# Three half chunks instead of two turned by VectorE, and products of E one pair later

## The chip, the cores and the metric

One core of a Trainium2 chip runs the whole program. The metric is the time of one execution in device microseconds, as the median of several runs. Some names: TensorE is PE in the profile (its weight loads are PEld), VectorE is DVE, ScalarE is ACT, GpSimd is POOL, SyncE is SP; SP issues nearly all transfers, and they run on the core's 16 DMA engines.

## The reference, cut to what matters

Four graph layers over 5120 nodes with 64 features share one dense 5120 x 5120 matrix `adj` of float32 (105 MB). Each layer normalises `x`, and then:

```python
# layer 0, with e made from the normalised x
h = adj @ (adj.T @ e)
x = x + layernorm(h) * gamma + beta + h_in
# layer 1:  x = x + adj @ h
# layer 2:  out = h @ w0; T1 = adj @ h; T2 = 2 adj @ T1 - h; T3 = 2 adj @ T2 - T1; x = x + (out + ...) + bias
# layer 3:  degree = sum of each row of (adj + I); x = x + relu(d * (adj + I) * d @ (h @ W + b))
```

The change touches layer 0 alone. There `adj` is needed both as it lies in memory (for `adj.T @ e`) and turned (for `adj @ t`). The later layers need only the turned form.

## The kernel before, in words

`adj` has 10 blocks of 512 rows; two blocks make a pair of rows, so there are 5 pairs (`ROWS`). The columns are cut into 7 groups g (`NG`): groups 0 to 5 have 768 columns (6 chunks of 128), the last has 512 (4 chunks). All work of layer 0 goes group by group, and in a group pair by pair.

For every pair (g, m):

- SP loads the two blocks of the pair into `raw` (1.5 MB each, `load_next`, L582; 1 MB each for group 6). `raw` holds one whole group, so block m of group g+1 may be loaded only when block m of group g has been turned and its row sums taken.
- The pair is turned into `staged`. Each chunk of 128 columns gives two half chunks, so a pair has 12. From the third pair on (`VECTOR_FROM`) TensorE turns ten of them, four 128 x 128 transposes each (`turn_banks`, L673), through four banks of PSUM (`turned`), and ScalarE copies each bank into `staged` (`copy_banks`, L879). VectorE turns the last chunk, that is two half chunks, straight from `raw` into `staged` with 16 transposes of 32-row blocks (`turn_chunk`, L1129).
- SP stores the turned pair, 3 MB, to `adj_t` in HBM (`store`, L570). `staged` has room for two pairs, so pair p may be turned into it only when the store of pair p - 2 has landed and its products are done (`wait_stage_free`).
- TensorE multiplies the turned pair with `t_cur`, the part of `adj.T @ E` of this group (`product_for_h`, L640), into `acc`, and VectorE adds that to `h_acc` (`add_h`, L1083).
- TensorE multiplies both raw blocks of the same pair of the next group with `E` into `t_acc` (`products_for_t`, L651). After the last one ScalarE copies `t_acc` out (L914), TensorE turns it (L716) and ScalarE writes `t_cur` (L931).

Row sums of the raw blocks (`sum_rows`) are taken by ScalarE (L923) or VectorE (L1040). Those of groups 1 to 5 are ScalarE's. Of group 6, VectorE takes one for each pair while group 5 is worked on, and two at the start of group 6.

Everything is ordered by hand. In iteration (g, i) of `group(g)` TensorE does: turn the next pair, multiply pair (g, i) with `t_cur`, multiply pair i of group g + 1 with `E`. VectorE does: turn its part of the next pair, its row sums if any, then `add_h(g, i)`. ScalarE does: copy the banks of the next pair, then its row sums. SP does: load the first block (g+1, 2m) after `wait_turned`, which asks for TensorE's and for VectorE's part of the turning, then store the pair, then load the second block. All three stand in one queue of SP, and each waits for those ahead of it. Group 6 has an order of its own (`last_group`), in units of half a pair; nothing in it is turned by VectorE, and it begins when `adj.T @ E` of group 6 is complete. After it come the passes of the later layers, whose tiles are loaded from `adj_t` (L588).

Of the kernel before, what the change touches and what calls it, by code (L numbers as in the profile page):

```python
# [33 lines left out]
PASSES = 5  # L34
MOVED_BANK = 3
VECTOR_FROM, VECTOR_LAST = 2, 0
VECTOR_CHUNKS = 1
EARLY_SLOTS = 1
LATE_SLOTS = 4
SLOTS = EARLY_SLOTS + NB + LATE_SLOTS  # L40
# [196 lines left out]
def gnn_stack(nc, x_d, adj_d, wu_d, du_d, pu_d, wi_d, di_d, pi_d, gam_d, bet_d, w2_d, b2_d, w3_d, b3_d, out_d):  # L237
    plan = Plan()
    ctx = ExitStack()
    with ctx:  # L240
# [178 lines left out]
        def chunks(g):  # L419

            return CHUNKS_LAST if g == NG - 1 else CHUNKS
# [36 lines left out]
        def by_vector(g, m):  # L458

            return m < VECTOR_LAST if g == NG - 1 else pair_no(g, m) >= VECTOR_FROM  # L460

        def banks(g, m):

            return range(2 * chunks(g) - 2 * VECTOR_CHUNKS * by_vector(g, m))

        def is_moved(g, m, j):

# [167 lines left out]
        def _(pe):  # L635
# [9 lines left out]
            def products_for_t(g, m):  # L645

                pe.wait_ge(raw_in[m], g * 16 + 16)
                columns = chunks(g) * P // 2
                for a in range(SUB):
                    for h in range(2):  # L650
                        last = nc.tensor.matmul(t_acc[h * D:(h + 1) * D, 0:columns], E[:, m * SUB + a, :],  # L651
                                                raw_of(g, m)[:, a, h * columns:(h + 1) * columns],
                                                start=(m == 0 and a == 0), stop=(m == NB - 1 and a == SUB - 1))
                if m == NB - 1:
                    last.then_inc(t_done, 1)
# [8 lines left out]
            def turn_banks(g, m, some):  # L664

                for j in some:
                    n = TURN_NO[g, m, j]
                    if n >= TURN_BANKS:
                        wait_bank(TURNS[n - TURN_BANKS])
                    c, h = divmod(j, 2)  # L670
                    for a in range(SUB):
                        b, sub = divmod(2 * a + h, SUB)
                        last = nc.tensor.transpose(turned[n % TURN_BANKS][:, a * P:(a + 1) * P],  # L673
                                                   raw_of(g, 2 * m + b)[:, sub, c * P:(c + 1) * P], ident[:, :])
                    last.then_inc(chunk_turned, 1)
# [61 lines left out]
            def group(g):  # L737
                for i in range(ROWS):
                    after = (g, i + 1) if i + 1 < ROWS else (g + 1, 0)
                    begun = BEGUN if (g, i) == (0, 0) else 0  # L740
                    turn_banks(*after, range(begun, TURN_BANKS))
                    if i == 0:
                        turn_t(g)
                    turn_banks(*after, banks(*after)[TURN_BANKS:])
                    if i == 0:
                        pe.wait_ge(t_ready, g + 1)
                    wait_copied(pe, g, i)
                    for u in (2 * i, 2 * i + 1):
                        product_for_h(g, u)
                    for m in (2 * i, 2 * i + 1):  # L750
                        products_for_t(g + 1, m)

            def last_group():
                g = NG - 1
                for u in range(UNITS):
                    if u + 2 < UNITS:
                        turn_unit(g, u + 2, range(CHUNKS_LAST))
                    if u == 0:
                        turn_t(g)
                        pe.wait_ge(t_ready, g + 1)  # L760
                    if u >= 2 and u % 2 == 0:
                        rows_of_h(u // 2 - 1)
                    wait_copied(pe, NG - 1, u // 2, u % 2)
                    product_for_h(g, u)
# [252 lines left out]
        def _(dve):  # L1017
# [94 lines left out]
            def turn_chunk(g, m):  # L1112

                if by_vector(g, m):
                    for b in range(2):
                        dve.wait_ge(raw_in[2 * m + b], g * 16 + 16)
                    if g < NG - 1:
                        wait_stage_free(dve, g, m)
                    elif m >= 1:
                        wait_turned(dve, g, m - 1)  # L1120
                    else:
                        wait_turned(dve, g - 1, ROWS - 1)
                    half, c = chunks(g) // 2, chunks(g) - 1
                    rows = raw_flat if g < NG - 1 else raw_flat[:, 0:NB * SUB * CHUNKS_LAST * P]
                    src = rows[:, :].rearrange("p (m a h k) -> p m h a k", m=ROWS, h=2, k=chunks(g) * P)[:, m]
                    dst = turned_into(g, 2 * m + 1)[:, (half - 1) * PAIR:half * PAIR].rearrange("p (h a n) -> p h a n", h=2, a=SUB)
                    for q in range(4):
                        for b in range(4):
                            last = nc.vector.transpose(dst[b * SQ:(b + 1) * SQ, :, :, q * SQ:(q + 1) * SQ],  # L1129
                                                       src[q * SQ:(q + 1) * SQ, :, :, c * P + b * SQ:c * P + (b + 1) * SQ])  # L1130
                    last.then_inc(vector_turned, 1)

            def group(g):
# [189 lines left out]
```

## Time and profile before

| what | us |
|---|---|
| median of 3 runs (lowest, highest) | 1450.26 (1450.21, 1451.71) |
| the profiled execution's own time | 1449.24 |
| its span, first to last instruction | 1447.0 |
| PE busy | 1419.3 (98%) |
| DVE busy | 491.5 (34%) |
| ACT busy | 399.7 (28%) |
| POOL busy | 84.2 (6%) |
| TensorE's granted clock, share of full | 0.999 |

Busy time is what the engine's instructions cover; matmuls are pipelined and their ends are modelled, so a PE that is busy all the time is not at its peak. The span of 1447.0 us has two parts here: layer 0 with the turning, up to about 550 us, and the passes after it. DMA share is the mean busy share of the 16 DMA engines; since packets overlap a little it can read above 1.

### The profile page before, as it was taken

Reading aid. Unit: us, or ns where it says so; the run is one execution under the profiler, and the core shown is the slowest. Engines: PE = TensorE matmul, PEld = TensorE weight load, DVE = VectorE, ACT = ScalarE, POOL = GpSimd, SP = SyncE. Lnnn points to the kernel's source line nnn. Section 1 sums busy time; section 2 is a strip of 40 time slices with the busy share of each in tenths; the row PEclk is TensorE's granted clock in tenths of the full one; section 3 lists DMA queues with packets and bytes.
Section 4 is the critical chain, followed back from the end, with each engine's and each line's share of the span. In section 5 each row is a group of like instructions: output and inputs, shape, how many; then the busy total and the mean of one; then the engine's idle time right before and its main releaser. Section 6 shows DMA issues by size and latency. Waiting matters only on the chain.

```text
span 1447.0 us, 18473 instructions
## 1 busy us (share of the span) xinstructions
PE 1419.3 (98%) x7601; PEld 600.1 (41%) x7601; DVE 491.5 (34%) x1082; ACT 399.7 (28%) x885; POOL 84.2 (6%) x67
## 2 busy tenths in 40 slices
PE   6999999999999999999999999999999999999998
PEld 3555555555555563333333333333333333333332
DVE  6684544545546533331132211011311121101044
ACT  2378777777776551000000000000000000000000
POOL 2210000000000037000000000000000000000000
PEclk9999999999999999999999999999999999999999
DMA  9999999999999998999996797899797848996998
GB/s 322 392 417 411 420 412 414 419 408 415 401 406 372 388 403 348 419 421 420 420 413 217 315 361 291 327 350 319 302 340 263 311 180 354 393 382 224 357 420 315
DMA packets 97607, 523.26 MB, mean 362 GB/s; under 512 B 18764, under 2 KB 18804, under 8 KB 54644
## 3 DMA queue, kind: packets, MB, share of 16 engines
q1 hardware_dynamic: 90436, 520.40, 91.3%
q10 hardware_dynamic: 7088, 1.67, 0.5%
q8 instruction: 61, 1.00, 0.3%
q14 instruction: 22, 0.18, 0.0%
HBM read 415.88 MB, written 106.17 MB: 361 GB/s over the span
## 4 chain that ended last, share of the span: by engine, by line
PE 61%; DMA 2%; DVE 1%; POOL 0%; issue 0%; ACT 0%; DVEq 0%
PE turned L640 33%; PE acc L640 25%; DMA over_wide<-adj_t 2%; PE turned L673 1%; PE turned L825 1%; PE t_rows L809 0%; PE turned L831 0%; DVE staged L1169 0%; PE t_acc L799 0%; PE t_acc L725 0%; PE t_rows L725 0%; POOL rstd L1272 0%; DVE staged L1035 0%; DVE staged L1025 0%; DVE staged L1231 0%
## 5 line engine op out<-in xcount | busy, mean ns | idle before, releaser
L1129 DVE STREAM_TRANSPOSE staged<-raw 32x256 f32<-32x256 f32 x448 | 194.9, 435 | 5.8
L651 PE MATMUL t_acc<-raw,E 128*64 128x384 f32 (+1 forms) x1120 | 184.4, 476 | 5.7 <-DMA raw<-in_adj_dram 5.7
L879 ACT ACTIVATE staged<-turned 128x512 f32<-128x512 f32 x303 | 152.7, 640 | 105.7 <-PE turned L673 105.2
L923 ACT ACTIVATE t_t<-raw 128x768 uint8<-128x768 f32 (+1 forms) x216 | 177.2, 902 | 0.0
L640 PE MATMUL acc<-staged,t_cur 128*64 128x512 f32 x720 | 161.1, 596 | 0.0
L673 PE MATMUL turned<-ident,raw 128*128 128x128 f32 x1376 | 160.2, 274 | 0.0
L673 PEld LDWEIGHTS turned<-ident,raw 128*128 128x128 f32 x1376 | 149.7, 140 | 24.9 <-issue 24.9
L640 PE MATMUL turned<-over_last,C 128*64 128x512 f32 x672 | 152.1, 592 | 0.0
L651 PEld LDWEIGHTS t_acc<-raw,E 128*64 128x64 f32 x1120 | 78.3, 138 | 109.4 <-issue 86.0
L1272 POOL TENSOR_TENSOR rstd<-rstd,minus_half 128x8 f32<-128x8 f32 (+1 forms) x30 | 44.2, 1473 | 1267.1 <-DVE rstd L1031 1267.1
L640 PE MATMUL turned<-over_last,R 128*64 128x512 f32 x512 | 116.5, 593 | 0.0
L640 PE MATMUL acc<-over_last,R 128*64 128x512 f32 x440 | 99.9, 593 | 0.0
L987 ACT ACTIVATE part<-turned 128x512 f32<-128x512 f32 x12 | 7.2, 597 | 313.1 <-PE turned L640 287.3
L1169 DVE STREAM_TRANSPOSE staged<-staged 32x128 f32<-32x128 f32 x304 | 91.9, 302 | 4.5
L640 PEld LDWEIGHTS turned<-over_last,C 128*64 128x64 f32 x672 | 48.2, 137 | 95.5 <-issue 95.5
L1083 DVE TENSOR_TENSOR h_acc<-acc,h_acc 128x512 f32<-128x512 f32 x30 | 20.8, 692 | 197.2 <-PE acc L640 197.2
L640 PEld LDWEIGHTS acc<-staged,t_cur 128*64 128x64 f32 x720 | 49.0, 137 | 90.8 <-issue 90.8
L640 PE MATMUL acc<-over_last,C 128*64 128x512 f32 x384 | 86.6, 592 | 0.0
L1243 DVE TENSOR_TENSOR staged<-turned,part 128x512 f32<-128x512 f32 x11 | 7.6, 692 | 225.8 <-PE turned L640 191.7
L640 PE MATMUL turned<-over_last,E 128*64 128x512 f32 x320 | 74.1, 593 | 0.0
L640 PEld LDWEIGHTS turned<-over_last,R 128*64 128x64 f32 x512 | 36.2, 137 | 71.2 <-issue 69.4
L855 ACT ACTIVATE staged<-staged 128x512 f32<-128x512 f32 x10 | 6.3, 630 | 206.0 <-DVE staged L1025 206.0
(139 smaller groups left out, 1062.9 us busy)
## 6 DMA issues: line engine op xcount, KB each, us to landing
over_last<-adj_t SPq DMA_DIRECT2D x181, 1024.0 KB, 8.9
staged<-adj_t SPq DMA_DIRECT2D x91, 1024.0 KB, 9.5
raw<-in_adj_dram SPq DMA_DIRECT2D x60, 1536.0 KB, 19.7
adj_t<-staged SPq DMA_DIRECT2D x30, 3072.0 KB, 18.1
over_wide<-adj_t SPq DMA_DIRECT2D x23, 1024.0 KB, 7.6
raw<-in_adj_dram SPq DMA_DIRECT2D x10, 1024.0 KB, 14.8
adj_t<-over_last SPq DMA_DIRECT2D x8, 1024.0 KB, 12.1
adj_t<-C SPq DMA_DIRECT2D x2, 1024.0 KB, 21.7
```

The costliest lines, as they stand in the source:

```text
L640: last = nc.tensor.matmul(bank[h * D:(h + 1) * D, :], v[:, t + c, :], tile[:, (2 * c + h) * B:(2 * c + h + 1) * B], start=start and c == 0 ...
L651: last = nc.tensor.matmul(t_acc[h * D:(h + 1) * D, 0:columns], E[:, m * SUB + a, :], raw_of(g, m)[:, a, h * columns:(h + 1) * columns], st ...
L673: last = nc.tensor.transpose(turned[n % TURN_BANKS][:, a * P:(a + 1) * P], raw_of(g, 2 * m + b)[:, sub, c * P:(c + 1) * P], ident[:, :])
L825: last = nc.tensor.matmul(weigh_bank[odd][:, i * 4 * D:(i + 1) * 4 * D], feat_t[rows, nodes], w0123[rows, :, :].rearrange("p w d -> p (w d ...
L879: nc.scalar.activation(turned_into(g, u)[:, i * B:(i + 1) * B], turned[n % TURN_BANKS][:, :], ACT.Copy) \
L923: nc.scalar.activation(passed[n % 2][:, 0:chunks(g) * P], raw_of(g, m)[:, a, :], ACT.Copy, accum_out=deg_part[:, m * SUB + a, g:g + 1]).th ...
L987: nc.scalar.activation(part[:, m, :], open_bank[plan.bank["dual", p, m]], ACT.Copy).then_inc(part_saved, 1)
L1083: ins = nc.vector.tensor_tensor(h_acc[:, m, :], acc[pair % 2][:, :], h_acc[:, m, :], ALU.add)
L1129: last = nc.vector.transpose(dst[b * SQ:(b + 1) * SQ, :, :, q * SQ:(q + 1) * SQ], src[q * SQ:(q + 1) * SQ, :, :, c * P + b * SQ:c * P + (b ...
L1169: last = nc.vector.transpose(dst[b * SQ:(b + 1) * SQ, :, h, e, :], src[q * SQ:(q + 1) * SQ, :, b, :])
L1243: ins = nc.vector.tensor_tensor(y_sb[r % 2], bank, part[:, m, :], ALU.add)
L1272: op.tensor_tensor(v, v, minus_half[:, t(0)], ALU.pow).then_inc(pow_ready, 1)
```

## The change: what it does

`VECTOR_CHUNKS` goes. A new `vector_banks(g, m)` says how many half chunks of a pair are VectorE's: 3 in groups 1 to 5, 2 in group 0 (pairs from the third on) and none in group 6. TensorE turns the rest (`banks`): 9 half chunks instead of 10 for the 25 pairs of groups 1 to 5. VectorE does the whole last chunk as before, then the second half of the chunk before it with 16 more transposes of half the width.

TensorE's products of `E` with pair i of group g + 1 move from iteration (g, i) to iteration (g, i + 1). Those of the last pair (blocks `NB - 2` and `NB - 1`) move to the start of the next group, ahead of the turning there; that is the same place in TensorE's order as before, but the products of the pair before now stand directly ahead of them.

```diff
+        def vector_banks(g, m):
+            if not by_vector(g, m):
+                return 0
+            return 3 if 0 < g < NG - 1 else 2
+
         def banks(g, m):
-            return range(2 * chunks(g) - 2 * VECTOR_CHUNKS * by_vector(g, m))
+            return range(2 * chunks(g) - vector_banks(g, m))
...
                 for i in range(ROWS):
                     after = (g, i + 1) if i + 1 < ROWS else (g + 1, 0)
                     begun = BEGUN if (g, i) == (0, 0) else 0
+                    if i == 0 and g > 0:
+                        products_for_t(g, NB - 2)
+                        products_for_t(g, NB - 1)
                     turn_banks(*after, range(begun, TURN_BANKS))
...
                     for u in (2 * i, 2 * i + 1):
                         product_for_h(g, u)
-                    for m in (2 * i, 2 * i + 1):
-                        products_for_t(g + 1, m)
+                    if i > 0:
+                        products_for_t(g + 1, 2 * i - 2)
+                        products_for_t(g + 1, 2 * i - 1)
 
             def last_group():
                 g = NG - 1
+                products_for_t(g, NB - 2)
+                products_for_t(g, NB - 1)
...
-                    half, c = chunks(g) // 2, chunks(g) - 1
...
-                    dst = turned_into(g, 2 * m + 1)[:, (half - 1) * PAIR:half * PAIR].rearrange("p (h a n) -> p h a n", h=2, a=SUB)
-                    for q in range(4):
-                        for b in range(4):
-                            last = nc.vector.transpose(dst[b * SQ:(b + 1) * SQ, :, :, q * SQ:(q + 1) * SQ],
-                                                       src[q * SQ:(q + 1) * SQ, :, :, c * P + b * SQ:c * P + (b + 1) * SQ])
+                    half = chunks(g) // 2
+                    left = vector_banks(g, m)
+                    c = chunks(g) - 1
+                    while left > 0:
+                        at = (c - half) * PAIR
+                        dst = turned_into(g, 2 * m + 1)[:, at:at + PAIR].rearrange("p (h a n) -> p h a n", h=2, a=SUB)
+                        for q in range(4):
+                            for b in range(4):
+                                to = dst[b * SQ:(b + 1) * SQ, :, :, q * SQ:(q + 1) * SQ]
+                                of_raw = src[q * SQ:(q + 1) * SQ, :, :, c * P + b * SQ:c * P + (b + 1) * SQ]
+                                if left == 1:
+                                    to, of_raw = to[:, 1], of_raw[:, 1]
+                                last = nc.vector.transpose(to, of_raw)
+                        left, c = left - 2, c - 1
                     last.then_inc(vector_turned, 1)
```

## Rows read from the trace of the kernel before

**Rows 1.** The page: data rate in 40 slices of 36.2 us.

```profile
GB/s 322 392 417 411 420 412 414 419 408 415 401 406 372 388 403 348 419 421 420 420 413 217 315 361 291 327 350 319 302 340 263 311 180 354 393 382 224 357 420 315
```

**Rows 2.** Windows between stores' issues: length, busy per engine, clock, DMA share, GB/s.

```profile
94.52:169.74 75.22, 75.22 (x485) 41.64 (x483) 41.68 (x87) 58.65 (x133) 0.00 (x0) 1.00 1.02 416
169.74:261.67 91.93, 90.86 (x581) 49.64 (x579) 45.41 (x102) 70.21 (x159) 0.00 (x0) 1.00 1.02 415
261.67:431.38 169.71, 167.71 (x1064) 90.77 (x1062) 83.23 (x187) 128.86 (x291) 0.00 (x0) 1.00 1.01 410
431.38:488.84 57.46, 55.78 (x389) 33.17 (x387) 36.67 (x71) 38.81 (x91) 0.00 (x0) 1.00 0.98 373
```

**Rows 3.** Timeline of PE, one pair of group 3: start, length, work, [idle before].

```profile
327.16 2.75 PE L651 MATMUL t_acc<-raw,E 128*64 128x384 f32 x16
330.09 2.80 PE L651 MATMUL t_acc<-raw,E 128*64 128x384 f32 x16 [0.18 <-DMA raw<-in_adj_dram]
332.82 4.59 PE L673 MATMUL turned<-ident,raw 128*128 128x128 f32 x40
337.34 5.37 PE L640 MATMUL acc<-staged,t_cur 128*64 128x512 f32 x24
```

**Rows 4.** Waits from 80 to 508 us: total us, times, longest.

```profile
PE t_acc L651 <- DMA raw<-in_adj_dram: 4.7, 15, 0.9
```

**Rows 5.** Timeline of SP's queue in the same pair.

```profile
337.44 0.37 SPq L582 DMA_DIRECT2D raw<-in_adj_dram  x1
338.55 0.34 SPq L570 DMA_DIRECT2D adj_t<-staged  x1
338.99 0.37 SPq L582 DMA_DIRECT2D raw<-in_adj_dram  x1
```

**Rows 6.** DMA issues at 337.44, 338.55, 338.99: size, us from issue to landing.

```profile
raw<-in_adj_dram SPq DMA_DIRECT2D x1, 1536.0 KB, 11.9
adj_t<-staged SPq DMA_DIRECT2D x1, 3072.0 KB, 18.4
raw<-in_adj_dram SPq DMA_DIRECT2D x1, 1536.0 KB, 21.8
```

**Rows 7.** Lines: form, count, busy us, mean ns (L1169 from 787 to 793 us).

```profile
L1169 DVE STREAM_TRANSPOSE staged<-staged 32x128 f32<-32x128 f32 x16 | 4.8, 302 | 0.2
L673 PE MATMUL turned<-ident,raw 128*128 128x128 f32 x1376 | 160.2, 274 | 0.0
```

**Rows 8.** Timeline of DVE in group 5.

```profile
451.53 0.69 DVE L1083 TENSOR_TENSOR h_acc<-acc,h_acc 128x512 f32<-128x512 f32 x1 [8.16 <-PE acc L640]
452.14 7.17 DVE L1129 STREAM_TRANSPOSE staged<-raw 32x256 f32<-32x256 f32 x16
459.35 2.29 DVE L1040 TENSOR_REDUCE deg_part<-raw 128x4 f32<-128x2048 f32 x1
```

**Rows 9.** Timelines of SP's queue and PE at the end of group 5.

```profile
487.73 0.37 SPq L582 DMA_DIRECT2D raw<-in_adj_dram  x1
488.84 0.65 SPq L570 DMA_DIRECT2D adj_t<-staged  x1
489.59 0.38 SPq L582 DMA_DIRECT2D raw<-in_adj_dram  x1
508.08 1.95 PE L651 MATMUL t_acc<-raw,E 128*64 128x256 f32 x16 [0.96 <-DMA raw<-in_adj_dram]
```

**Rows 10.** DMA issues at 475.46, 487.73, 488.84, 489.59 and, alone in the queue, 1150.45.

```profile
raw<-in_adj_dram SPq DMA_DIRECT2D x1, 1024.0 KB, 18.9
raw<-in_adj_dram SPq DMA_DIRECT2D x1, 1024.0 KB, 9.4
adj_t<-staged SPq DMA_DIRECT2D x1, 3072.0 KB, 15.8
raw<-in_adj_dram SPq DMA_DIRECT2D x1, 1024.0 KB, 18.4
staged<-adj_t SPq DMA_DIRECT2D x1, 1024.0 KB, 4.7
```

More of the change, by code:

```diff
@@ L36 @@
 VECTOR_FROM, VECTOR_LAST = 2, 0
-VECTOR_CHUNKS = 1
 EARLY_SLOTS = 1
```

## The prediction

> **What bounds the kernel now.** The page says PE 98% busy, and one would stop there. The data rate by slices [rows 1] says something else: until slice 12 the transfers run near the 419 to 421 GB/s that the load-only stretch from slice 17 on reaches. So I cut layer 0 into windows that begin and end at issues of a store, one store per pair [rows 2]. The first holds 5 pairs (15.04 us each), the next 6 (15.32), the third 11 (15.43), the fourth, group 5 with its smaller loads, 4 (14.37). The DMA share is 1.01 to 1.02 in the first three, 0.98 in the fourth.
>
> Next PE's timeline of one pair [rows 3]. Steps start 4.52 us apart for the 40 transposes (332.82 to 337.34), about 5.2 for the 24 products with `t_cur` (5.37 long, the next overlapping), and 5.66 for the 32 products with `E` (327.16 to 332.82), with a wait for a `raw` block between its halves. By itself PE needs the 15.04 us a pair of the first window, where it was busy for 75.22 of 75.22 us [rows 2]. Later it takes 15.4 for the same work, and what stops it are those waits for `raw`, 4.7 us in 15 pieces by the list of waits [rows 4], some more where only the weight loads waited.
>
> Is the block late because it was asked for late? SP's queue and the landings answer [rows 5, 6]. First load, store and second load are issued at 337.44, 338.55 and 338.99 and land at 349.3, 356.95 and 360.8; the second load of the pair before (same row, one period of 15.4 earlier) landed at 345.4. So the landings follow one another by 3.9, 7.6 and 3.9 us, 15.4 together, and the first load stood in the queue for 8.0 us before its turn. The queue is never empty: PE is held to the pace of the transfers, 6.29 MB a pair, and was near it before. That is the bound from about 200 us to the end of group 5.
>
> The phase ends with it too [rows 9, 10]: the last raw load of group 6 is issued at 489.59 and lands at 508.0, and PE, idle for 0.96 us, starts its last products with `E` at 508.08. `t_cur` of group 6, and all that follows, hang on this landing.
>
> **The change part by part.** *Transposes and copies taken away.* 25 pairs lose 4 transposes each, 100 in all, at 4.52 / 40 = 0.113 us: 11.3 us of PE (by busy time per instruction, 160.2 / 1376 = 0.116, 11.6 us) [rows 3, 7]. PE then needs 15.04 - 0.45 = 14.6 us a pair. ScalarE loses 25 copies. What hides it: the transfers at 15.1 to 15.4 a pair. Value on the path: 0. Its bounds are 0 and -11.6 us, the second if PE were the bound. I take 0 since the nearest row, 8.0 us of queue ahead of each first load, excludes that earlier turning lands anything earlier.
>
> *Products of E one pair later.* Nothing is added or removed; PE has a pair more before it needs a block, so its 4.7 us of waits go [rows 4]. What is late next: `staged` has two places, so turning pair p waits for the landing of store p - 2, and this comes at the transfers' pace. Blocks of the last pair keep their place, so the wait at 508.08 stays. Value 0, bounds 0 and -4.7 us.
>
> *VectorE's third half chunk.* 16 transposes of 32x128. The form stands in the passes: 302 ns each, 16 in 4.8 us busy plus 0.2 idle, 5.0 us [rows 7]; the source there lies closer together than the stretches of `raw` do, and the 16 of twice the width take 7.17 [rows 8], so between 4.8 and 7.2 us. I take 5.0; turning is then 12.2 us. Who waits: `last` releases SP, where first load, store and second load of the pair stand behind `wait_turned`, and PE's products with `t_cur`.
>
> In groups 1 to 4 VectorE has 12.2 + 0.7 of 15.4 us, and starts when the store two pairs before has landed. Counted from there, the queue still holds second load, first load, store, second load: 3.9 + 3.9 + 7.6 + 3.9 = 19.3 us [rows 6]. The load that waits for VectorE is issued at 12.2, 7 us ahead of need. At a group's start PE has two pairs of products in a row, then none; VectorE waits for `add_h` about 1.5 us longer there, which leaves over 3 us even with ScalarE's row sums in the way. Cost 0; if that cover were gone, each us late is a us of the end.
>
> Group 5 is different: loads are 1 MB, VectorE also sums rows, and the queue is shorter. VectorE needs 12.2 + 2.3 + 0.6 = 15.1 us a pair [rows 8] where the transfers need 14.4 [rows 2]. Its chain: `add_h(5,0)` ends at 451.53 + 0.69 = 452.2, less 0.5 since PE turns one half chunk less just before, 451.7. Turning (5,2) ends at 463.9, (5,3) at 479.0, (5,4) at 494.1; the second sets the load of 479.1, which the queue reaches at about 481, the third the first load of the last pair, 494.2 instead of 487.73 [rows 9]. The queue reaches it when the load of 475.46 has landed, 494.4 [rows 10], so it is issued just as its turn comes, and a load into an empty queue takes 4.7 us from issue to landing for 1 MB [rows 10], against 2.7 for one in line (494.4 to 487.73 + 9.4 = 497.1). It lands at 494.2 + 4.7 = 498.9, up to 499.2 as its packets are smaller. The store takes 7.5 us in line (497.1 to 488.84 + 15.8 = 504.6), the last load 3.4 (to 489.59 + 18.4 = 508.0). So the end is 499.0 + 7.5 + 3.4 = 509.9, less 0.2 because engines that ran dry start together: 509.7, against 508.0. Cost +1.7 us. Bounds: 0, where the queue holds, and +8: 16 transposes at 7.2 us instead of 5.0 add 2.2 in each of three turnings, 6.6, less what the queue still hides.
>
> The added instructions are 16 for VectorE in each pair; they and PE's 8 fewer (weight loads too) leave the work of the queue as it was, 0.
>
> **Sum.** 0 + 0 + 0 + 1.7 on the profiled 1449.24 us (span 1447.0 and 2.2 around it): 1450.9. The median is 1.0 above the profiled execution, so 1450.26 + 1.7 = 1452.0 us.
>
> A rule that speaks against "transfers are at their limit": the Trainium skill, DMA: Bandwidth & Descriptors, Specifications, gives 435 GB/s as the ceiling of the fabric. By it a pair's 6.29 MB would take 14.5 us, PE at 15.0 would have been the bound all along, and PE's saving would come through, up to 11 us. The windows show 410 to 416 GB/s at a share over 1, so the measurement decides; the rule adds weight to the fourth rival alone.
>
> **The rivals.**
>
> *A, the forecast:* groups 1 to 4 unchanged, group 5 gives 1 to 3 us back. 1452.0, its own range 1450 to 1454.
>
> *B, slower:* VectorE's chain in group 5 lets the queue run dry for two pairs. It decides once the turning takes over 12.6 us or so: then the load at 479.1 is late as well, and each dry spell costs 4.7 - 2.7 = 2.0 us on top of the lag. With 13 us a turning: 3 x 0.8 + 2.0 more, 1452.0 + 4.4, about 1456. For it: the strided source, and 2 us between 479.1 and 481, which is just what a load needs to start. Against: 302 ns is a measured form, and engines are in line long before.
>
> *C, faster:* the pace of 15.4 instead of 15.1 is itself a consequence of PE's waits, and goes with them. The 11 pairs of the third window at 15.04 instead of 15.43 and the 6 of the second instead of 15.32 [rows 2] give 4.3 + 1.7 = 6.0, less 1.7 in group 5: 1446.0. For it: the first window ran at 15.04 with the same packets [rows 2]. Against: loads stand 8.0 us in line, so no wait of PE reaches the transfers.
>
> *D, faster:* PE is the bound, as the page's 98% has it. 11.3 us and the 4.7 of waits, 16 together, at least the 11.3: 1434 to 1439. Against: every row of the queue.
>
> *E, nothing:* the change takes and gives nothing that ends up on the path, VectorE being hidden in group 5 as well: 1450.3. It is also the case that the change doesn't do what it says for the time.
>
> **How the numbers follow.** No change means within 0.2%, 2.9 us, so 1447.4 to 1453.2. A has 0.52, of which 0.07 lies over 1453.2; B 0.17; C 0.14, of which 0.12 is under 1447.4; D 0.05; E 0.12. Faster: 0.17. Slower: 0.07 + 0.17 = 0.24. No change: 0.59. The range 1445.5 to 1456 leaves out D, a third of C and nearly half of B, 0.05 + 0.05 + 0.07.
>
> **What would show it.** Windows of groups 1 to 4 with 15.3 to 15.5 us a pair and a share over 1, PE's waits there turned from `raw` into waits for ScalarE's copies, that is for a store, and no or few waits for `raw` inside a group; VectorE's 32 transposes in 12.2 us; in group 5 a first load of the last pair issued at about 494 and the last landing at 509.7. C shows as pairs of 15.1 us in group 3, D as pairs of 14.5. I am wrong if the last landing comes before 507 or after 512, or if the passes, which nothing here touches, change by more than 1 us.

## The result, and the profile after

| | median of runs (lowest, highest) | profiled execution | its span | clock |
|---|---|---|---|---|
| before | 1450.26 (1449.39, 1452.03), 11 runs | 1449.24 | 1447.0 | 0.999 |
| after | 1458.7 (1453.91, 1461.57), 11 runs | 1455.46 | 1453.7 | 0.995 |

The ratio is 1.0053 (95%: 1.0044 to 1.0062): slower by about 8 us (6.4 to 9.0), where 1452.0 with a range of 1445.5 to 1456.0 was predicted. The profiled execution of after lies in the lower part of its runs; the places of the loss can be read from it, the size comes from the medians. The experiments have 5 to 11 timed runs each; in their sessions before had 1450.8, and differences are taken from that.

The page after, its totals, its data rate (36.3 us a slice) and the group of VectorE's transposes:

```profile
PE 1412.3 (97%) x7501; PEld 591.8 (41%) x7501; DVE 613.9 (42%) x1482; ACT 387.3 (27%) x860; POOL 84.3 (6%) x67
...
GB/s 320 395 416 412 408 404 399 413 374 411 417 413 359 365 417 360 420 421 420 420 420 201 322 358 295 349 330 316 298 351 264 302 185 360 387 380 230 352 419 316
...
L1148 DVE STREAM_TRANSPOSE staged<-raw 32x256 f32<-32x256 f32 (+1 forms) x848 | 316.4, 373 | 49.0 <-DMA adj_t<-staged 37.8
```

The work moved as written: PE has 7 us less, VectorE 122 us more. But nine of the slices 3 to 14 carry less than in [rows 1], 359 and 365 in slices 13 and 14 against 372 and 388; only slices 4, 11 and 12 carry more.

Windows between the same stores as in [rows 2], with 5, 6, 11 and 4 pairs (length, busy per engine, clock, DMA share, GB/s):

```profile
91.47:169.86 78.39, 77.37 (x487) 41.12 (x485) 64.07 (x152) 60.17 (x139) 0.00 (x0) 1.00 1.01 409
169.86:265.17 95.31, 91.20 (x573) 48.28 (x571) 74.98 (x199) 68.19 (x156) 0.00 (x0) 1.00 1.01 406
265.17:435.44 170.27, 164.40 (x1016) 87.09 (x1014) 137.36 (x364) 123.38 (x279) 0.00 (x0) 0.98 1.01 405
435.44:497.63 62.19, 57.91 (x401) 33.87 (x397) 54.14 (x135) 33.05 (x79) 0.00 (x0) 1.00 0.95 364
```

They come to 15.7, 15.9, 15.5 and 15.5 us a pair instead of 15.04, 15.32, 15.43 and 14.37. Their borders are issues, and an issue may come early and land at the old time: the first window begins 3 us earlier than before's for that reason. Landings tell it more cleanly. The last raw block of each group landed at (us, from the transfers in both traces):

| end of group | 0 | 1 | 2 | 3 | 4 | 5 |
|---|---|---|---|---|---|---|
| before | 130.3 | 207.4 | 283.9 | 360.8 | 438.5 | 508.0 |
| after | 130.5 | 208.8 | 286.9 | 365.3 | 441.5 | 514.2 |

Of the 6.7 us that the span grew, 6.2 are there at the last landing: 3.0 gathered in groups 1 to 4, of which I had said 0, and 3.2 in group 5, of which I had said 1.7. The rest is TensorE's slower start after its last wait; what follows it is within 1 us of before.

The net hides two opposite movements. Add up the gaps between landings for each kind of transfer (first load, store, second load of a pair). In groups 1 to 4 the 20 first loads took 84.2 us against before's 77.9, but the 20 stores took 149.1 against 152.4. In group 5 the first loads took 21.4 against 14.5, the second loads 13.4 against 16.8. So late first loads cost 13.2 us in all, and other transfers that landed more quickly gave 7 of them back. Many stores land 7.3 us behind their forerunner and many 7.6, in every trace; what decides between the two, no run here separates. In group 4 after even gained 1.5 us on before.

Waits of after from 80 to 521 us (total us, times, longest):

```profile
DVE staged L1148 <- DMA adj_t<-staged: 37.8, 17, 3.8
DVE h_acc L1094 <- PE acc L645: 26.1, 6, 6.9
...
PE t_acc L656 <- DMA raw<-in_adj_dram: 11.7, 5, 3.8
...
PE turned L678 <- ACT staged L890: 5.7, 6, 1.0
```

Inside a group PE's small waits for `raw` are gone, as predicted. In their place stand five large ones, 11.7 us against the 4.7 of [rows 4], one at the end of each of groups 1 to 5, where the blocks of the last pair keep their old place. One of them in PE's timeline (start, length, work, [idle before]):

```profile
276.02 7.91 PE L656 MATMUL t_acc<-raw,E 128*64 128x384 f32 x48
286.92 5.39 PE L656 MATMUL t_acc<-raw,E 128*64 128x384 f32 x16 [3.00 <-DMA raw<-in_adj_dram]
292.24 2.26 PE L678 MATMUL turned<-ident,raw 128*128 128x128 f32 x16
...
294.66 2.35 PE L678 MATMUL turned<-ident,raw 128*128 128x128 f32 x20
296.94 5.37 PE L645 MATMUL acc<-staged,t_cur 128*64 128x512 f32 x24
```

So the lateness of the transfers is saved up over a group and paid in one piece. What makes them late is seen on the two sides of one late load. VectorE, and SP's queue, at the start of group 3:

```profile
283.21 12.24 DVE L1148 STREAM_TRANSPOSE staged<-raw 32x256 f32<-32x256 f32 x32 [2.77 <-DMA adj_t<-staged]
302.36 0.69 DVE L1094 TENSOR_TENSOR h_acc<-acc,h_acc 128x512 f32<-128x512 f32 x1 [6.91 <-PE acc L645]
302.96 12.24 DVE L1148 STREAM_TRANSPOSE staged<-raw 32x256 f32<-32x256 f32 x32
```

```profile
298.59 17.04 SPq L587 DMA_DIRECT2D raw<-in_adj_dram  x2
315.72 0.46 SPq L575 DMA_DIRECT2D adj_t<-staged  x1
```

PE had two pairs of products with `E` to do in a row (276.02 to 292.3), then turned, and only then came to the products with `t_cur` (296.94). `add_h` hangs on these, and VectorE's next turning stands behind `add_h`. It stood idle for 6.9 us (the longest of six such waits, 26.1 us in all) and turned from 302.96 to 315.2. The store that freed its place had landed at 298.1, so the start was 4.9 us later than the transfers allowed. The next load was issued at 315.3 (the last 0.37 us of the piece beginning at 298.59), while the load ahead of it, issued at 298.59, landed 19.3 us later, at 317.9. It had 2.7 us in line. It landed 7.6 us after its issue, at 322.9, that is 4.9 us after its forerunner and not the 3.9 of the full queue [rows 6].

VectorE in group 5:

```profile
454.14 0.69 DVE L1094 TENSOR_TENSOR h_acc<-acc,h_acc 128x512 f32<-128x512 f32 x1 [4.08 <-PE acc L645]
454.75 12.23 DVE L1148 STREAM_TRANSPOSE staged<-raw 32x256 f32<-32x256 f32 x32
467.01 2.29 DVE L1051 TENSOR_REDUCE deg_part<-raw 128x4 f32<-128x2048 f32 x1
469.21 0.68 DVE L1094 TENSOR_TENSOR h_acc<-acc,h_acc 128x512 f32<-128x512 f32 x1
469.81 12.23 DVE L1148 STREAM_TRANSPOSE staged<-raw 32x256 f32<-32x256 f32 x32
...
484.87 12.23 DVE L1148 STREAM_TRANSPOSE staged<-raw 32x256 f32<-32x256 f32 x32
```

SP's queue there, and PE at the end:

```profile
483.12 14.41 SPq L587 DMA_DIRECT2D raw<-in_adj_dram  x2
497.63 0.46 SPq L575 DMA_DIRECT2D adj_t<-staged  x1
```

```profile
514.26 3.25 PE L656 MATMUL t_acc<-raw,E 128*64 128x256 f32 x16 [3.78 <-DMA raw<-in_adj_dram]
```

The chain of turning, sums and `add_h`, 15.06 us a pair (454.75, 469.81, 484.87), has the lengths that I gave it. It began 3.1 us later than forecast (454.75 instead of 451.7), and group 5 itself had begun 3.0 us late. The first load of the last pair was issued at 497.17 instead of 494.2 and landed 6.4 us later, at 503.6, where 4.7 were counted [rows 10].

### The profile page after: what moved, and what is told of

It is laid out like the page before. It is cut to its first block, busy times and chain, and to the rows that moved or that the text cites. A ratio compares the mean times of both kernels' runs of the same rounds, so it can differ in the third digit from the quotient of the medians.

```text
span 1453.7 us, 18648 instructions
## 1 busy us (share of the span) xinstructions
PE 1412.3 (97%) x7501; PEld 591.8 (41%) x7501; DVE 613.9 (42%) x1482; ACT 387.3 (27%) x860; POOL 84.3 (6%) x67
## 4 chain that ended last, share of the span: by engine, by line
PE 61%; DVE 2%; POOL 0%; issue 0%; ACT 0%; DVEq 0%
PE turned L645 33%; PE acc L645 26%; DVE staged L1188 1%; PE turned L678 1%; PE turned L836 1%; PE t_rows L820 0%; PE turned L842 0%; POOL rstd L1291 0%; PE t_acc L810 0%; PE t_acc L730 0%; DVE staged L1046 0%; DVE staged L1036 0%; DVE X L1234 0%; DVE staged L1264 0%; DVE rstd L1041 0%; DVE total L1035 0%
## 5 line engine op out<-in xcount | busy, mean ns | idle before, releaser
L1148 DVE STREAM_TRANSPOSE staged<-raw 32x256 f32<-32x256 f32 (+1 forms) x848 | 316.4, 373 | 49.0 <-DMA adj_t<-staged 37.8
L656 PE MATMUL t_acc<-raw,E 128*64 128x384 f32 (+1 forms) x1120 | 183.9, 481 | 11.7 <-DMA raw<-in_adj_dram 11.7
L890 ACT ACTIVATE staged<-turned 128x512 f32<-128x512 f32 x278 | 140.7, 642 | 80.2 <-PE turned L678 79.8
L678 PE MATMUL turned<-ident,raw 128*128 128x128 f32 x1276 | 153.2, 277 | 7.6 <-ACT staged L890 5.7
L678 PEld LDWEIGHTS turned<-ident,raw 128*128 128x128 f32 x1276 | 138.7, 141 | 39.0 <-issue 27.4
L1262 DVE TENSOR_TENSOR staged<-acc,part 128x512 f32<-128x512 f32 x8 | 5.5, 691 | 151.5 <-PE acc L645 83.3
L645 PEld LDWEIGHTS turned<-over_last,R 128*64 128x64 f32 x512 | 36.2, 137 | 71.2 <-issue 70.6
## 6 DMA issues: line engine op xcount, KB each, us to landing
raw<-in_adj_dram SPq DMA_DIRECT2D x10, 1024.0 KB, 12.3
```

The costliest lines, as they stand in the source:

```text
L645: last = nc.tensor.matmul(bank[h * D:(h + 1) * D, :], v[:, t + c, :], tile[:, (2 * c + h) * B:(2 * c + h + 1) * B], start=start and c == 0 ...
L890: nc.scalar.activation(turned_into(g, u)[:, i * B:(i + 1) * B], turned[n % TURN_BANKS][:, :], ACT.Copy) \
L1148: last = nc.vector.transpose(to, of_raw)
L1262: ins = nc.vector.tensor_tensor(y_sb[r % 2], bank, part[:, m, :], ALU.add)
```

## The experiments

"Time in line" of a first load is from its issue to the landing of the second load ahead of it, from each trace's transfers.

**The change in parts.** `e1_products_only` moves the products and leaves VectorE its two half chunks; `e2_third_only` does the other part alone; `e3_two_in_group5` and `f5_three_in_group5` cut the third half chunk by groups.

```diff
 e1:  return 3 if 0 < g < NG - 1 else 2   ->   return 2
 e2:  vector_banks as in after; products of E in iteration (g, i), as before
 e3:  return 3 if 0 < g < NG - 1 else 2   ->   return 3 if 0 < g < NG - 2 else 2
 f5:  return 3 if 0 < g < NG - 1 else 2   ->   return 3 if g == NG - 2 else 2
```

> The changed kernel with two half chunks for VectorE in every group: only the move of the products of E is left. Theory V (VectorE's longer turning releases the loads late and thins the queue): close to the kernel before, 1449 to 1452 us, first loads again 7 to 8 us in line inside a group. Rival P (the uneven order of TensorE, with two pairs of products in a row at a group's end and the idle wait there, is what costs): most of the loss is here, 1454 to 1459 us, with waits for raw of 2 to 4 us at each group's end and a lower granted clock behind them.

> The kernel before with three half chunks for VectorE in groups 1 to 5 and the products of E left in their place. Theory V: most of the loss is here, 1454 to 1459 us, VectorE 15.1 us a pair in group 5 and the last raw load landing 3 us or more late. Rival P: 1449 to 1452 us, as TensorE's order is even.

> The changed kernel with two half chunks for VectorE in group 5 as well as in group 0, three in groups 1 to 4. Theory V with the split read off the two traces (3 us lost in groups 1 to 4, 3.4 us in group 5): 3 to 4 us less than the changed kernel, about 1454 to 1455 us. If group 5 has no part in it: 1458 us. If it is all of it: 1450 to 1451 us.

> The changed kernel with three half chunks for VectorE in group 5 alone, two in all other groups. If the two costs add (4.4 us in groups 1 to 4, 6.6 us in group 5, over e1_products_only): 1454 us. If group 5 costs more only because it starts late: nearer to the 1.7 us of the forecast, 1449 to 1450 us.

| kernel | median us (lowest, highest) | ratio to before (95%) | last raw landing |
|---|---|---|---|
| e1_products_only | 1447.64 (1447.25, 1448.84) | 0.998 (0.9971, 0.9989) | 505.9 |
| e2_third_only | 1463.12 (1461.01, 1466.17) | 1.0087 (1.0074, 1.0101) | 525.0 |
| e3_two_in_group5 | 1452.06 (1450.01, 1455.32) | 1.001 (1.0001, 1.0019) | 510.1 |
| f5_three_in_group5 | 1453.1 (1451.77, 1454.66) | 1.0019 (1.001, 1.0028) | 511.3 |

The move of the products is a gain of 3.1 us by itself, and the third half chunk is the whole loss. On top of the move it costs 4.4 us in groups 1 to 4 (e3 less e1) and 5.5 in group 5 (f5 less e1); 1447.6 + 4.4 + 5.5 = 1457.5 leaves 1.2 of after's 1458.7, which is inside the spread of the runs. f5 also settles why group 5 costs more than forecast: its group 5 began on time (landing 437.5 at the end of group 4, e1 has 437.4), and it lost the 5.5 us all the same. Without the move it costs more, 12.3 us (e2 less before): PE then waits for the late block in the same iteration, 25.0 us in 21 pieces in that trace. The expectations had the signs right but not all sizes: e1 came out 1.4 us under its range, e2 4 us over its own, e3 2 us under.

What the move changes is in its trace. PE at the end of group 5, and the waits from 80 to 521 us:

```profile
501.09 7.08 PE L656 MATMUL t_acc<-raw,E 128*64 128x256 f32 x64
508.10 1.97 PE L678 MATMUL turned<-ident,raw 128*128 128x128 f32 x16
```

```profile
DVE staged L1148 <- DMA adj_t<-staged: 33.8, 19, 2.6
...
DVE deg_part L1051 <- DMA raw<-in_adj_dram: 1.8, 1, 1.8
...
PEld t_acc L656 <- DMA raw<-in_adj_dram: 0.2, 1, 0.2
```

PE waits for no `raw` block any more, at the end neither: the 0.96 us of [rows 9] is gone. VectorE, which in before's trace never waited for a store's landing, but 26 times and 188.5 us for the products of `add_h`, waits 19 times for such a landing and 156.8 us for products: it begins to turn as soon as its place is free. With it the time in line of most first loads rises from 7 to 8 us to 9 to 12.

That the longer line brought the 3.1 us is not shown. In groups 1 to 4 of before none of the 20 first loads was late (all gaps 3.9 us), so there was nothing to gain by it. The profiled e1 has its last landing 2.1 us earlier. Its stores of groups 1 to 4 took 149.9 us instead of 152.4 and its second loads of group 5 15.4 instead of 16.8, while its first loads took 2.5 us more. Why those transfers landed more quickly stays open.

**Is it the time on TensorE or the time on VectorE?** `e4_vector_late` is before with 16 half-width transposes done a second time by VectorE in groups 1 to 5, ahead of the release of SP; PE keeps all its work. `e5_spare_tensor` is before with PE's and ScalarE's part cut as in after and VectorE's as in before: one half chunk of each pair of groups 1 to 5 is left unturned. `f2_spare_moved` is the same on e1.

```diff
 e4, behind the 16 transposes of a chunk in before:
+                    if 0 < g < NG - 1:
+                        chain.step(last)
+                        for q in range(4):
+                            for b in range(4):
...
+                                last = nc.vector.transpose(to[:, 1], of_raw[:, 1])
 e5:
-            return range(2 * chunks(g) - 2 * VECTOR_CHUNKS * by_vector(g, m))
+            return range(2 * chunks(g) - 2 * VECTOR_CHUNKS * by_vector(g, m) - (0 < g < NG - 1))
 f2, with vector_banks as in e1:
-            return range(2 * chunks(g) - vector_banks(g, m))
+            return range(2 * chunks(g) - vector_banks(g, m) - (0 < g < NG - 1))
```

> The kernel before, TensorE and ScalarE unchanged, but VectorE does the 16 half-width transposes of its last half chunk twice in groups 1 to 5, so that it releases each pair about 5.1 us later and TensorE is spared nothing. Theory V: the loss comes back without any other part of the change, 1454 to 1460 us. Rival P, or a theory by which the loss comes from TensorE getting ahead: 1450 to 1452 us.

> The kernel before, but in groups 1 to 5 TensorE and ScalarE leave one more half chunk of each pair unturned and nobody turns it (that part of the turned matrix is stale); VectorE as before. It is the saving of the change without its price. The forecast's term is 0: 1450 to 1451 us. If TensorE is the bound: 1435 to 1439 us. From the 2.4 us between e4_vector_late and e2_third_only: about 1448 us.

> e1_products_only, with one half chunk of each pair of groups 1 to 5 left out as in e5_spare_tensor (stale there). Theory V: with the products moved TensorE has slack except in group 5, where it no longer waits for raw; so 1 to 2 us of it come through: 1445.5 to 1447 us. If TensorE had become the bound everywhere once the products are moved: about 11 us less, 1436 us.

| kernel | median us (lowest, highest) | ratio to before (95%) |
|---|---|---|
| e4_vector_late | 1465.54 (1463.47, 1469.97) | 1.0105 (1.009, 1.012) |
| e5_spare_tensor | 1448.85 (1447.62, 1450.28) | 0.9985 (0.9977, 0.9994) |
| f2_spare_moved | 1445.47 (1444.69, 1446.84) | 0.9966 (0.9952, 0.9979) |

VectorE's lateness is enough: with nothing taken from PE the same 16 transposes cost 14.7 us. And PE's saving of 11.3 us of work is worth 1.9 us (e5) or 2.2 (f2 less e1) at the end; e4 less e2 gives 2.4, but the runs of those two overlap. e4 came out 5 us over its range. The fourth rival, PE as the bound, has its own experiment in e5 and falls with it.

**How much lateness costs how much?** `d1_late_by_8` and `d2_late_by_16` are e1 with 8 or 16 of the repeated transposes (2.5 and 5.1 us), so that the lateness alone differs.

```diff
 as in e4, with AGAIN = 2 (d1) or 4 (d2)
+                        for q in range(AGAIN):
+                            for b in range(4):
```

> e1_products_only, but VectorE does 8 of its half-width transposes again in groups 1 to 5, 2.5 us a pair. Theory L (what costs is the time a first load stands in line falling under about 6 us; more line is worth nothing): in groups 1 to 4 loads still stand 6 to 9 us in line and nothing is lost there; in group 5 some fall under 6: 1 to 3 us over e1_products_only, 1448.5 to 1450.5 us. If lateness costs in proportion (half of d2): about 1454 us.

> The same with 16 transposes again, 5.1 us a pair: VectorE as long as in the changed kernel, TensorE spared nothing. Theory L: the changed kernel without its 2 us from TensorE's saving, 1460 to 1462 us, of which 5 to 6 us in group 5. A rival by which the third half chunk costs through what it reads and writes, and not through its length: near e1_products_only, 1448 to 1450 us.

| lateness | median us (lowest, highest) | over e1 | time in line in group 5, pairs 0 to 4 |
|---|---|---|---|
| 0 (e1) | 1447.64 | | 11.7 4.7 7.1 9.1 8.1 |
| 2.5 (d1) | 1449.36 (1447.03, 1451.49) | 1.7 | 9.2 5.9 4.2 6.4 6.5 |
| 5.1 (d2) | 1457.65 (1456.79, 1462.48) | 10.0 | 6.7 4.4 1.6 2.5 2.1 |

The first 2.5 us cost 1.7, the next 2.6 cost 8.3. A cost that grew with the number of transposes (their reads and writes, the extra instructions) would have given 5.0 for the first half, where 1.7 was measured; that rival falls. The cost sets in late. In d2 VectorE is as long as in after and TensorE is spared nothing, yet the two times (1457.65 and 1458.7) can't be told apart; so in after PE's saving is worth nothing that can be measured. d2 had been expected at 1460 to 1462.

**Where does it set in?** The 14 traces hold 280 first loads of groups 1 to 4. In line, the gap to the landing ahead is 3.9 us:

| time in line, us | loads | mean gap, us | share with a gap over 4.1 |
|---|---|---|---|
| under 4 | 9 | 5.38 | all |
| 4 to 5 | 14 | 4.89 | 79% |
| 5 to 6 | 25 | 4.52 | 56% |
| 6 to 7 | 74 | 4.11 | 23% |
| 7 to 8 | 59 | 3.91 | 3% |
| over 8 | 99 | 3.90 | about 1% |

From about 7 us in line a first load lands in time; from 6 to 7 us three in four do. Before had 7 to 8 us, so it had a slack of 1 or 2 us at most, where I had read nearly all of its 8.0 us as slack. After has

| pair | 0 | 1 | 2 | 3 | 4 |
|---|---|---|---|---|---|
| group 1 | 6.5 | 6.1 | 4.7 | 7.7 | 8.0 |
| group 3 | 7.1 | 4.9 | 2.7 | 6.8 | 6.4 |
| group 5 | 6.6 | 4.4 | 1.8 | 1.4 | 1.3 |

In the first three pairs of a group it falls, since `add_h` comes late there; in groups 1 to 4 it recovers afterwards, as VectorE has 12.9 us of work in a pair of 15.4. In group 5 it does not: VectorE's 15.06 us are more than the transfers' 14.4, and the gaps are 2.6, 4.1, 4.6, 5.0 and 5.1 us where 2.7 is the gap in line.

**VectorE's period or VectorE's delay, in group 5?** `h1_sums_by_scalar` is after with group 6's row sums, as far as they fall into group 5, given to ScalarE, so that the period is 12.9 us while a turning stays at 12.2.

```diff
-        ACT_SUMS = [x for x in PAIR_SUMS if 0 < x[0] < NG - 1 or x[0] == NG - 1 and x[1] % 2 == 1 and x[1] < NB - 2]
+        ACT_SUMS = [x for x in PAIR_SUMS if 0 < x[0] < NG - 1 or x[0] == NG - 1 and x[1] < NB - 2]
```

> The changed kernel, but the row sums of group 6 that VectorE takes during group 5 are ScalarE's; VectorE then needs 12.9 us a pair there instead of 15.1, under the pace of the transfers. If its period is what costs in group 5: most of the 5.5 us come back, 1453.5 to 1455 us. If it is the 12.2 us between the start of its turning and the loads: about 1458 us.

Measured: 1456.09 (1455.14 to 1459.69), ratio 1.004 (1.0028 to 1.0052). VectorE in group 5, with the sums gone and a wait for a store in their place:

```profile
468.95 12.23 DVE L1148 STREAM_TRANSPOSE staged<-raw 32x256 f32<-32x256 f32 x32
...
482.90 12.24 DVE L1148 STREAM_TRANSPOSE staged<-raw 32x256 f32<-32x256 f32 x32 [1.00 <-DMA adj_t<-staged]
```

The time in line in group 5 becomes 6.7, 4.4, 2.0, 4.1 and 4.7 us: the fall after the third pair is gone, and the fall up to the third pair stays. The time is 2.6 us less by the medians, but the runs of the two kernels overlap and so do their ratios' intervals, so this gain is not clear of the noise. In the traces group 5 took 71.5 us from first to last landing, against 72.7 in after and 68.5 in e1. So VectorE's period is at most about half of the term of group 5, in the traces nearer to a quarter (1.2 of 4.2 us), and the rest is the delay up to the third pair.

**Can the start of a group be made shorter?** `g1_half_move` has two half chunks and moves one block's products of each pair alone, so that PE has three blocks in a row at a group's start and not four. `a1_half_move_third` is the same with the third half chunk.

```diff
 g1 against e1, and a1 against after:
                     if i == 0 and g > 0:
-                        products_for_t(g, NB - 2)
                         products_for_t(g, NB - 1)
...
                     if i > 0:
-                        products_for_t(g + 1, 2 * i - 2)
                         products_for_t(g + 1, 2 * i - 1)
+                    products_for_t(g + 1, 2 * i)
```

> Two half chunks for VectorE everywhere, and of the products of E with a pair only the second block's stand one pair later; the first block's keep their place. The second loads are the ones TensorE waited for, and TensorE's order is less uneven at a group's end, so the load after it should stand about 9 us in line instead of 6.9. Theory V: 1446 to 1448 us, equal to e1_products_only or a little less. If what helps in e1_products_only is the slack of the first block too: 1448 to 1450 us.

> The changed kernel with only the second blocks' products moved, as in g1_half_move. TensorE then waits less in one piece at a group's end, and the load after it is released earlier. Theory L: loads in groups 1 to 4 gain up to 2 us of line where they have 3 to 5 now: 1455 to 1458 us. If the idle wait at a group's end and the clock behind it had no part: 1458 to 1459 us.

g1: 1447.03 (1446.04 to 1448.94), ratio 0.9978 (0.9968 to 0.9988). a1: 1459.56 (1457.24 to 1463.58), 1.0058 (1.0045 to 1.0071). In groups 2 to 4 of g1 the second pair has 7.6 to 7.7 us in line instead of e1's 6.2 to 6.9, and the third 9.8 to 10.1 instead of 8.8 to 9.4, which is the direction expected (in group 1 it has 6.4 and 8.3, less than e1); in the time it can't be told from e1. With the third half chunk the line did not grow as expected, a1 lies over its range of 1455 to 1458, and it can't be told from after's 1458.7; in group 5 the third pair has 0.6 us in line, the fourth 1.3, the fifth 0.8. g1 and e1 are both faster than before and after; g1, 3.8 us under before's 1450.8, is the best version that does all the work.

## Why the prediction was wrong, point by point

**The bound** was read rightly. The transfers' queue sets the pace from group 1 to group 5, and the last raw landing carries the end: after's span is longer by 6.7 us, 6.2 of them by this landing. One step on the way was not sound: that PE "by itself" needs 15.04 us a pair. In f2 PE has 0.45 us less to do in each pair and its group 1 still took 75.5 us, 15.1 a pair. The first window was at the transfers' pace too, with stores that land 7.3 us behind the load and not 7.6.

**Transposes and copies taken away, value 0:** they are worth about 2 us while loads are released in time (e5, f2), and nothing in after. The reason that I gave, 8.0 us of queue ahead of each load, excluded any gain by an earlier release; e5 shows that there was a little. A size, within its bounds of 0 and -11.6.

**Products of E one pair later, value 0:** measured -3.1 (e1), within 0 and -4.7. I let PE's waits for `raw` go and did not ask what else waits for PE. In before VectorE never waited for a store's landing, in e1 19 times: PE's waits did reach the release of the loads, by way of the products with `t_cur`, `add_h` and the next turning. Rival C had said so. Half of its 6.0 us came, but that they came in its way is not shown, since no first load of before's groups 1 to 4 was late.

**VectorE's third half chunk, groups 1 to 4, "Cost 0":** this is the step that failed. Measured 4.4 us (e3 less e1). Two things were wrong in it. "Issued at 12.2, 7 us ahead of need" took any load issued ahead of its turn to be free, with 2 us (4.7 less 2.7) as all that a load needs to start. By the 280 loads it needs about 7. And I put the delay of `add_h` at a group's start at 1.5 us; in group 3 VectorE's turning began 4.9 us behind the landing that freed its place (302.96 and 298.1, above), since two pairs of products stand ahead of everything there. I wrote "over 3 us left"; the third pair of group 3 had 2.7, so this count was nearly right. What I made of it, "cost 0", was not.

**Group 5, +1.7:** measured 5.5 (f5 less e1). The mechanism, VectorE's 15.1 us against 14.4, was right and is in the trace to 0.1 us. What failed is the same step as in groups 1 to 4: a load was counted as late only once it was issued behind its turn. In after the loads of the last three pairs, with 1.8, 1.4 and 1.3 us in line, were late every time (gaps of 4.6, 5.0 and 5.1), and the last took 6.4 us and not the 4.7 of one that starts alone [rows 10]. The late start of group 5 in after is not the reason: in f5 VectorE's chain began at 451.03 (forecast 451.7), the last pair's first load was issued at 493.46 (forecast 494.2), and the last landing came at 511.3 (forecast 509.7). Of the sum's small terms, neither the allowance for smaller packets (0.1 us in the sum) nor the 0.2 us taken off because engines that ran dry start together is shown by any run; in after the packets behind a dry spell took longer than before it (last section).

**The rivals.** B has the right sign and, for 5.5 us, the right place, and its mechanism, a turning that lets the queue run short in group 5, was at work; for the 4.4 us of groups 1 to 4 it had nothing. Its point of decision, 12.6 us of turning, was not right: a turning of 12.24 was enough. I made it hang on the duration of the transposes, which I had nearly exactly, and not on how long a load has to stand in line. D is refuted by e5, E by the result. Slower had 0.24 in all, and after's 1458.7 lies above the whole range, since no rival had a cost in groups 1 to 4.

**The page's rule.** The Trainium skill, DMA: Bandwidth & Descriptors, Specifications, has 435 GB/s as the fabric's ceiling. By it PE would be the bound. The traces don't bear that out as a pace that is held: the stretch of mixed loads and stores never passed 420 in a slice of 36 us [rows 1] or 416 in a window of 57 us and more [rows 2], though single stretches of a few us read more (451 below), and PE's 11.3 us less brought 2.

## What to carry to other kernels

A queue that is "never empty" has no slack by that alone: measure how long each load stands in line, find in the trace at what time in line the gaps begin to grow, and price every delay of a release against that. Where an engine has both to release a buffer and to follow another engine, moving work between them is priced by the latest release in a group, not by the mean. And when a move of work in time makes one engine's waits vanish, ask which other engine stood behind these waits; here the move was worth 3.1 us, where the 11 us of work taken away were worth 2, though by which way is not shown.

## What the runs showed of the hardware

A load of 1.5 MB needed about 7 us between its issue and the landing ahead of it to land at the queue's pace; with 4 to 5 us it came 1.0 us late on the average, with under 4 it came 1.5 us late (table above). Over 30 us the DMA share moves by a few hundredths only, while the rate falls, in equal stretches of before, then after:

```profile
300.00:330.00 30.00, 29.73 (x190) 16.05 (x186) 14.69 (x34) 23.11 (x52) 0.00 (x0) 1.00 1.02 413
```

```profile
300.00:330.00 30.00, 28.98 (x180) 15.16 (x178) 25.53 (x67) 26.73 (x62) 0.00 (x0) 1.00 0.97 377
150.00:180.00 30.00, 30.00 (x192) 16.05 (x190) 25.39 (x68) 23.27 (x53) 0.00 (x0) 1.00 1.01 399
```

From 150 to 180 us before has 416 GB/s at a share of 1.02, after 399 at 1.01: packets of the loads took 133 ns on the average there, against 125 in before. Cut finer, around the late load of above (issued at 315.3, its forerunner landing at 317.9), the share falls too:

```profile
314.00:316.00 2.00, 2.00 (x16) 0.93 (x14) 1.93 (x6) 1.65 (x5) 0.00 (x0) 1.00 0.61 244
316.00:318.00 2.00, 2.00 (x16) 0.73 (x12) 1.95 (x5) 0.00 (x0) 0.00 (x0) 1.00 0.89 229
```

In before the same stage, the last us ahead of a forerunner's landing at 314.7, reads:

```profile
311.00:313.00 2.00, 2.00 (x14) 0.79 (x12) 1.00 (x2) 2.00 (x6) 0.00 (x0) 1.00 1.09 429
313.00:315.00 2.00, 1.82 (x12) 0.63 (x10) 1.93 (x6) 1.32 (x4) 0.00 (x0) 1.00 1.09 444
```

This shows what the time in line left out: the 16 engines are not in step. By the packets in after's trace, the forerunner kept 16 engines busy until 314.5 and then only 7 to 10 of them until 316.3, when the first packets of the late load began, 1.1 us after its issue. In before the fastest engines were a whole load ahead of the slowest: the load issued at 306.7 has its forerunner's landing at 314.7, but at 312.9 the first engine had already moved its share of that load and begun on the store behind it. A share takes 3.9 us (32 packets of 122 ns), so that engine had needed the load 5.6 us ahead of the forerunner's landing, and the issue 1.1 us before that: 6.7 us in line. This is an estimate from the rows of one pair, and it comes out at the table's 7. The spread differs by stage: in group 1 of before the first engine reached the store 0.3 to 0.6 us behind the forerunner's landing in four of five pairs, and 6.8 us in line were enough there.

Part of the lateness is a second thing. The load packets begun from 316 to 317.5 took 190 to 270 ns on the average, those before them 122. Over the 9 loads with under 4 us in line, an engine was idle for 0.85 us on the average around the forerunner's landing, and load packets took 155 ns, against 127 where a load had over 8 us.

TensorE's clock fell after the long waits. PE's wait of 3.00 us at 283.9 and what followed, then the one of 3.78 at 510.5:

```profile
284.00:287.00 3.00, 0.08 (x2) 0.08 (x4) 2.90 (x8) 0.00 (x0) 0.00 (x0) 0.84 1.06 406
287.00:292.00 5.00, 5.00 (x16) 1.61 (x16) 4.82 (x14) 0.00 (x0) 0.00 (x0) 0.50 1.07 451
292.00:300.00 8.00, 8.00 (x57) 5.60 (x56) 3.31 (x11) 7.27 (x16) 0.00 (x0) 0.94 0.92 349
...
514.00:518.00 4.00, 3.74 (x19) 2.11 (x20) 2.29 (x1) 0.38 (x1) 0.00 (x0) 0.59 1.01 422
```

At 0.50, the 1.2 GHz level, the 16 products with `E` took 5.39 us, where they take 2.75 to 2.80 at full clock [rows 3]; after a wait of 1.56 us, in group 4, the same 16 took 2.80. At 286.92 this adds up to 2.6 us to the delay of the third pair. It is not the main cause: e4 lost most of all, and its clock was 0.999.

What stays open: what sets how far the 16 engines are out of step, and why packets slow down behind a late load; why stores land 7.3 us behind the first load in some stages and 7.6 in others, which is where e1's groups 1 to 4 gained; how much of those groups' loss is the clock's; and why PE's saving, worth 2 us elsewhere, is not seen in after.
